# ViT tower with attention and experts: silu made in one ScalarE pass from the fourth shared chunk on

## What is computed

```python
scores = softmax(xf @ router_w); topk_scores, topk_idx = top_k(scores, 2)
g = einsum('nh,ehf->enf', xf, gate_w); u = einsum('nh,ehf->enf', xf, up_w)
y = einsum('enf,efh->enh', silu(g) * u, down_w)
routed = einsum('enh,ne->nh', y, combine)
shared = silu(xf @ shared_gate_w) * (xf @ shared_up_w) @ shared_down_w
out = layernorm(h + shared + routed)
```

## Time and profile before

| what | us |
|---|---|
| profiled execution | 790.15 |
| its span, first to last instruction | 788.4 |
| PE busy | 735.5 (93%) |
| VectorE busy | 539.5 (68%) |
| ScalarE busy | 419.5 (53%) |
| GpSimd busy | 159.2 (20%) |
| mean granted TensorE clock | 0.964 |

### The profile page before, as it was taken

How to read it: one execution, slowest core, us unless ns; L and a number is a source line. 1 busy time by engine, 2 the same in 40 slices (tenths; PEclk the granted TensorE clock), 3 DMA queues, 4 the chain that set the end, 5 groups by cost and what they waited for, 6 DMA issues and landing times. The chain is left out here.

```text
span 788.4 us, 14542 instructions
## 1 busy us (share of the span) xinstructions
PE 735.5 (93%) x5009; PEld 638.7 (81%) x5010; DVE 539.5 (68%) x1135; ACT 419.5 (53%) x779; POOL 159.2 (20%) x200
## 2 busy tenths in 40 slices
PE   5988999999999999999999979998988999999991
PEld 5867697979798897979797957886867999999881
DVE  0069898989798898979898988962651444444673
ACT  2365847565756758575756556211113555554254
POOL 2000000000000000000000000006743677775222
PEclk9999999999999999999999989788999999999986
DMA  8930001010102010010000033000001222221611
GB/s 286 313 127 25 11 24 45 23 45 23 45 0 66 2 51 18 23 34 23 12 23 12 16 116 105 24 22 19 0 3 44 75 86 82 80 87 42 247 67 57
DMA packets 28302, 47.35 MB, mean 60 GB/s; under 512 B 4793, under 2 KB 19107, under 8 KB 28274
## 3 DMA queue, kind: packets, MB, share of 16 engines
q1 hardware_dynamic: 22802, 37.24, 14.5%
q0 software_dynamic: 5472, 9.76, 4.0%
HBM read 35.57 MB, written 13.24 MB: 62 GB/s over the span
## 5 line engine op out<-in xcount | busy, mean ns | idle before, releaser
L572 POOL TENSOR_TENSOR rs<-ve,neg_half 111x2 f32<-111x2 f32 x11 | 12.4, 1130 | 491.3 <-DVE ve L1463 491.3
L743 PE MATMUL ps_X<-wkv_sb,hT 128*111 128x512 f32 (+1 forms) x176 | 85.7, 619 | 7.9 <-ACT v_sb L1115 7.4
L998 PE MATMUL ps_S<-attnT,v_sb 128*128 128x128 f32 x704 | 86.0, 275 | 1.3 <-ACT attnT L1237 0.8
L1382 DVE COPY_PREDICATED table<-bit,table 111x112 f32<-111x112 int16 (+6 forms) x110 | 76.3, 694 | 11.4 <-DVE table L1382 0.2
L998 PEld LDWEIGHTS ps_S<-attnT,v_sb 128*128 128x128 f32 x704 | 82.2, 192 | 1.8 <-ACT attnT L1237 1.0
L1066 ACT COPY simS<-ps_S 32x666 f32<-32x666 f32 (+3 forms) x105 | 74.1, 705 | 13.5 <-DVE table L1439 10.6
L743 PEld LDWEIGHTS ps_X<-wkv_sb,hT 128*111 128x111 f32 (+1 forms) x176 | 27.9, 174 | 50.7 <-issue 30.1
L1708 DVE COPY attnT<-ps_S 128x256 f32<-128x256 f32 x44 | 18.7, 424 | 71.1 <-PE ps_S L1012 71.1
L684 PE MATMUL ps_S<-hT,wq_sb 128*128 128x222 f32 (+1 forms) x352 | 66.3, 345 | 0.0
L684 PEld LDWEIGHTS ps_S<-hT,wq_sb 128*128 128x128 f32 x352 | 63.5, 190 | 0.1
L781 PE MATMUL ps_X<-oT,wout_sb 128*128 128x222 f32 x320 | 61.9, 350 | 0.0
(11 more groups left out here) (208 smaller groups left out, 1438.1 us busy)
## 6 DMA issues: line engine op xcount, KB each, us to landing
down_sb<-in_x_dram SPq DMA_DIRECT2D x10, 648.0 KB
gu_sb<-y_d SPq DMA_DIRECT2D x8, 512.0 KB, 6.9
h_d<-hT SPq DMA_DIRECT2D x11, 222.0 KB, 2.5
kept<-h_d SPq DMA_DIRECT2D x11, 222.0 KB, 2.6
h_d<-h SPq DMA_DIRECT2D x10, 222.0 KB
wkv_sb<-in_L_attn_Wkv_dram SPq DMA_DIRECT2D x2, 1024.0 KB, 10.2
gu_sb<-in_L_ffn_gate_w_dram SPq DMA_DIRECT2D x2, 1024.0 KB, 11.2
gu_sb<-in_L_ffn_up_w_dram SPq DMA_DIRECT2D x2, 1024.0 KB, 12.2
```

The lines of the kernel that those rows point to most:

```text
L743: mm = nc.tensor.matmul(X[:r, 1 - s], hT[:, k].rearrange("p b t -> p (b t)")[:, a * ROWS:a * ROWS + r], wkv_sb[:, k, INNER + 512 * s:INNER ...
L998: mm = nc.tensor.matmul(S[:, i, j * FF + f * P:j * FF + f * P + P], held[:, i, k, j, f * P:f * P + P], xgT[:, i, k], start=(k == 0), stop= ...
L1382: A.did(V.copy_predicated(near[:, :, :, 0:SL - d], by_side(bit[:, n], r)[:, :, :, 0:SL - d], near[:, :, :, d:SL]))
```

## The change

From chunk 3 on (`LATE = 3`) and in all 44 tiles ScalarE's pass is Silu in place of Tanh with scale 0.5, and VectorE makes one `tensor_tensor` product of its result and up, in place of two `scalar_tensor_tensor` steps. Chunks 0 to 2 stay as they were. ScalarE gets one more wait in the shared steps, for the product two steps back, which reads the buffer that it is about to write.

```diff
+        LATE = 3
...
             def shared_tanh(c, f):
                 w = chunks[c][1] * chunks[c][2]
                 act.wait_ge(sh_gu, c * FC + f + 1)
+                if c >= LATE:
+                    if f >= 2 or c > LATE:
+                        act.wait_ge(sh_hid, c * FC + f - 1)
+                    nc.scalar.activation(thS[:, f % 2, :w], S[:, f % 2, :w], ACT.Silu).then_inc(sh_tanh, 1)
+                    return
                 nc.scalar.activation(thS[:, f % 2, :w], S[:, f % 2, :w], ACT.Tanh, scale=0.5).then_inc(sh_tanh, 1)
...
             def tanh_tile(t, i):
                 act.wait_ge(tile_gu, t + 1)
-                nc.scalar.activation(thg[:, i], S[:, i, :FF], ACT.Tanh, scale=0.5).then_inc(tile_tanh, 1)
+                nc.scalar.activation(thg[:, i], S[:, i, :FF], ACT.Silu).then_inc(tile_tanh, 1)
...
                 dve.wait_ge(sh_tanh, c * FC + f + 1)
+                if c >= LATE:
+                    V.tensor_tensor(hidS[:, c % 2, f, :w], thS[:, i, :w], S[:, i, CHUNK:CHUNK + w], ALU.mult
+                                    ).then_inc(sh_hid, 1)
+                    return
...
             def hidden_tile(t, i):
                 dve.wait_ge(tile_tanh, t + 1)
-                V.scalar_tensor_tensor(sg[:, i], thg[:, i], 1.0, S[:, i, :FF], ALU.add, ALU.mult
-                                       ).then_inc(dve_tile, 1)
-                dve.wait_ge(dve_tile, t + 1)
-                V.scalar_tensor_tensor(hid[:, i], sg[:, i], 0.5, S[:, i, FF:], ALU.mult, ALU.mult
-                                       ).then_inc(tile_hid, 1)
+                V.tensor_tensor(hid[:, i], thg[:, i], S[:, i, FF:], ALU.mult).then_inc(tile_hid, 1)
```

## The result

| | before | after |
|---|---|---|
| median, us (20 runs each) | 790.27 | 787.63 |
| lowest and highest run | 787.90, 792.28 | 784.20, 790.80 |
| profiled execution, its span | 790.15, 788.4 | 786.21, 784.4 |
| mean granted TensorE clock | 0.964 | 0.971 |

The ratio of the times is 0.9964 with a 95% interval of 0.9952 to 0.9975: 2.8 us faster, between 2.0 and 3.8. That is within the 0.5% that the forecast named, but more than its 1.6 us.

A forecast was written before the change was run, and what follows sets the result against it. PE, busy 93%, was taken as the bound, with gains only where the pipeline fills, drains or runs short: 0.42 + 0.42 + 0.3 + 0.44 = 1.6 us. Forecast 790.96 - 1.6 = 789.4 us, range 787.1 to 791.4.

The forecast's parts named there:

- first tile: PE's second tile step, after 0.50 us idle: the product comes 0.42 us sooner and all of it counts.
- last tile: PE's last down matmuls of the tiles, after 0.79 us idle: 0.42 us gained, 0.37 us of waiting left.
- chunks 7 and 8: PE's weight loads wait 0.30 us once in each chunk; both stops go, 0.15 us each, 0.3 in all.
- chunk 9: PE stands 0.88 us before its last step for a product; two pairs in series to the end save 2 x 0.22 us.
- Middle of the tiles: nothing: Middle of the tiles: no gain, since the product is already 1.6 us early and PE is busy 20.00 of 20.00 us.
- Silu for Tanh at no cost: ScalarE's passes: Silu takes Tanh's time, 0.383 us on 256 columns; upper bound 0.61 us, cutting the gain to 1.0.
- The table load at no cost: Behind chunk 2's last Tanh: one load of 1.283 us fits in ScalarE's 5.24 us idle time, so costs nothing.
- part 4 of the forecast: ScalarE's new wait shares an instruction with the old one, asks for what has always happened, and costs 0.
- Chunks 3 to 5: nothing: Chunks 3 to 5: no gain, since PE would only run ahead to its 3.81 us wait for GpSimd's lists.
- PE's own matmuls would set the pace here too: Chunks 3 to 5: second reason for no gain, should the cover of PE's wait for the lists be gone.
- only the tiles gain: Rival: ScalarE's queue holds up the last steps in chunks 7 to 9, losing 0.74 us there; 790.1 us, chance 0.17.
- The clock stays up in chunk 9: Rival: shorter stops avert the clock fall in PE's last step, last rows start 0.97 us earlier; 788.4 us, chance 0.15.

The follow-up runs named there:

- tiles_bare: Kernel before with the one-pass silu in the 44 tiles alone, all chunks as before; ratio 1.0006 to the kernel before on chip 4.
- a_again: The changed kernel, unchanged, profiled a second time; ratio 0.9956 to the kernel before on chip 2.
- b_again: The kernel before, unchanged, profiled a second time; ratio 1.0009 on chip 2.
- c345_only: Silu and one product in chunks 3 to 5 alone, chunks 6 to 9 and tiles as before; ratio 0.9962 to the kernel before on chip 2.
- a_nop35: Changed kernel with an empty VectorE instruction in place of the old first step in chunks 3 to 5; ratio 0.9936 to the kernel before, chip 3.

## Why the prediction was right, and where it wasn't

- **The sum's own terms** came out one by one (shifts of the first table): first tile 0.44 (forecast 0.42), last tile 0.45 (0.42), chunks 7 and 8 0.16 and 0.17 (0.15 each), chunk 9 0.26 and 0.25 (0.22 each). Together 1.73 us against 1.6. The 27.96 and 27.63 us of chunks 6 to 8 repeat within 0.01 in all fourteen profiles, whatever the chip, and so do the 28.7 and 28.2 us of the end once clock falls are taken out.
- **"Middle of the tiles: nothing"** held: still 156 matmuls in 20.00 us. VectorE is busy 5.29 us there instead of 8.24, and the time went into its idle time ahead of the result copy, 89.7 us instead of 71.1:

```profile
640.00:660.00 20.00, 20.00 (x156) 18.93 (x155) 5.29 (x15) 12.03 (x22) 14.17 (x15) 1.00 0.26 83
```

- **Silu for Tanh at no cost** held (384 against 383 ns).
- **The table load at no cost** held, and for the reason given: it stood at 552.28, with 3.94 us of idle time left behind it. Where that cover was taken away, the load cost 1.42 us at PE. Timeline of ScalarE, after:

```profile
551.88 0.38 ACT L1223 ACTIVATE ex<-ps_S 128x256 f32<-128x256 f32 x1 [1.27 <-PE ps_S L843]
552.28 1.28 ACT L1221 ACT_TABLE_LOAD   x1
557.50 0.38 ACT L1221 ACTIVATE ex<-ps_S 128x256 f32<-128x256 f32 x1 [3.94 <-PE ps_S L843]
```

  The Trainium skill ("ScalarE: Activation LUTs", What ACT_TABLE_LOAD costs) adds a drain of about 1.38 us. Here the load follows the copy before it within 0.02 us and the Silu follows the load within 0.01 (tiles_bare above), so the load and what surrounds it took 1.31 us of ScalarE's time, no drain shows, and the measurement decides.
- **The new wait at no cost** held, but part 4 of the forecast reads the program wrongly: the wait does not share an instruction with the old one. The trace has 26 instructions EVENT_SEMAPHORE on ScalarE's sequencer (one for each step from chunk 3's third on) of 0.02 us. It costs nothing all the same: on chip 1 each pass of chunks 3 to 5 starts 0.04 us behind PE's step, with it as without.
- **"Chunks 3 to 5: nothing"** held on the chip that the forecast was made for, where PE waits 5.03 us for the lists and has no stop in these chunks. The two reasons beside it do not hold on the three other chips, where about 1 us is gained. "PE's own matmuls would set the pace here too" is wrong there: ScalarE's late pass and VectorE's product set PE's second step of chunk 5. And the scatters do take something from these products: VectorE computes their places behind the product of chunk 3's second step. On chip 1 these places are 0.44 us earlier too (7.21 and 6.77 us behind chunk 3's start), but there GpSimd is still busy with earlier scatters, one every 1.26 us, and does not wait for them.
- **Chunk 9** had the right price and half the reason. "For a product" named the last instruction of a chain; behind it stood 2 us of ScalarE's queue. The rival "only the tiles gain" was right that this queue holds PE up and wrong that the pair's 0.44 would then be lost: the pair is in series with it, as the forecast's argument against the rival said.
- **"The clock stays up in chunk 9"** did not come: the last step again took 1.97 us, and the window from 762 us shows half clock. In other profiles of either kernel the fall lands in the last down matmuls (a_again, 2.88 us instead of 1.91) or nowhere in the end (b_again). b_again and the profile of before are the same kernel, so where the fall lands differs from one execution to the next; it cancels only in a mean.
- **The size.** The forecast was 789.4 us and the median is 787.63. 0.7 us of the difference is the median before, 790.27 over 20 runs where three had given 790.96. The rest is a gain of 2.8 us where 1.7 can be pointed at. The profile pair has its other 2.25 us ahead of the tiles, nearly all in the gap behind the last scatter, and the forecast has no term for that: it took this gap as fixed. If the plain executions of the two kernels differ in this gap as their profiles do, it would more than fill the remaining 1.1 us (0.3 at the interval's lower end); only one profile of each was taken on this chip, so this stays open. The clock is the other candidate: among the changed kernel's 20 executions 0.01 more mean clock goes with 3.7 us less, and the clocks of the unchanged kernel's plain runs are not on record. The ratios on chips 2 and 3 also lie somewhat above the stretches, where the gap cannot be the reason: c345_only gained 3.1 us (at least 1.3) with 1.0 to 1.2 shown, a_nop35 5.3 (at least 2.8) with some 2.4 shown.

## What to carry to other kernels

Removing 28 us from an engine that is 68% busy gave 2.8 us. Such a change is worth what the few stops in which the bounding engine names that engine are worth, each up to about the length of the step removed, and on chip 1 these add up as read. (In chunk 5 on the other chips the stop was about twice the step, because VectorE's queue also stands ahead of the scatters.) A releaser's name is the end of a chain: before shortening the named step, look at what stood in the queue ahead of it. Here reordering that queue and one sum, with no work removed, gave 2.9 to 3.2 us, against 1.7 us for all stops that the whole change took away on chip 1. And a cover (a wait, an idle engine) belongs to a chip and a place as well as to a kernel: the load was free in one place and cost 1.4 us in another.

## What the runs showed of the hardware

- The same kernel takes 790 us on one chip and 819 to 824 on three others. In b_again 16.2 us are lost ahead of chunk 3 and 15.9 us in the tiles, ScalarE's waits for "remote" among them; 4.6 us come back in chunks 3 to 5, where PE does not wait for the lists. The granted clock is not the main part: the two profiles have 0.964 and 0.963, while over all executions of the changed kernel the mean is 0.968 on chip 1 and 0.958 on chip 2.
- On one chip the time of an execution goes with its mean granted clock: 0.01 more goes with 2.2, 4.8 and 3.0 us less among the 35, 29 and 27 executions of the unchanged kernel on chips 2, 3 and 4. Kernels with few executions should be compared at like clocks.
- The one table load that was not covered took 1.28 us, with 0.02 us ahead of it and 0.01 behind, and PE's next step came 1.42 us later. Silu came behind Exp and Tanh with one load, and Tanh, Square and the copies behind Silu with none.
- The time from the issue of the last indirect scatter to the indirect read that depends on it is near 4 or near 6 us. In all fourteen profiles it is the long one exactly where an instruction queue starts a block in between.
